# Value products of the second layer's first batch moved behind its last heads, more products of zeros before its norm, and the last FFN unit's factors put between a gate and its sum

## The reference, cut to what matters

```
h = layernorm(x) * (1 + ca) + sa
q = (h @ Wq.T + bq)            # 16 heads of 16
k = h @ Wk.T + bk              # one head of 16
v = h @ Wv.T + bv              # one head of 16
scores = q k^T * scale, masked to s < t; attn = softmax(scores); out = (attn v) @ Wo.T + bo
x = x + ga * out
h = layernorm(x) * (1 + cb) + sb
x = x + gb * (shared_ffn(h) + routed_ffn(h))
```

## Time and profile before

| What | Value |
|---|---|
| median of 3 runs | 636.39 us (634.04 to 637.16) |
| the profiled execution's own time | 634.54 us |
| its span, first to last instruction | 632.7 us |
| mean granted TensorE clock | 0.990 |
| busy share of PE, DVE, ACT | 93%, 58%, 46% |
| `filler` products of zeros (L703) | 28 in all |

### The profile page before, as it was taken

The page is one execution under the profiler, slowest core; times in us unless marked ns, Lnnn a source line. Parts: engine busy times, 40 slices in busy tenths (PEclk is TensorE's granted clock), DMA queues, the critical chain, the costliest instruction groups (busy, mean ns, idle before and its releaser), DMA issues.

```text
span 632.7 us, 10398 instructions
## 1 busy us (share of the span) xinstructions
PE 591.4 (93%) x3826; PEld 459.1 (73%) x3826; DVE 369.5 (58%) x725; ACT 291.6 (46%) x450; POOL 117.8 (19%) x90
## 2 busy tenths in 40 slices
PE   4898999998999999999999798889999999999995
PEld 3788645686898888888887465544447788888885
DVE  6477756755444545455557789893476523344456
ACT  3666775564323333333342563348763744333331
POOL 4400031223112222211230000003101331122220
PEclk9998999999999999999999799999999999999999
DMA  8464674000011111111100024402210000111101
GB/s 315 131 223 138 213 222 148 2 10 16 26 51 50 50 36 39 50 50 50 50 26 1 0 74 142 125 31 91 80 37 2 26 25 26 51 50 50 50 1 67
DMA packets 22195, 44.66 MB, mean 71 GB/s; under 512 B 3632, under 2 KB 7632, under 8 KB 22160
## 3 DMA queue, kind: packets, MB, share of 16 engines
q1 hardware_dynamic: 21840, 44.05, 21.9%
q10 hardware_dynamic: 320, 0.13, 0.1%
HBM read 33.16 MB, written 11.01 MB: 70 GB/s over the span
## 4 chain that ended last, share of the span: by engine, by line
PE 70%; DVE 19%; ACT 5%; DMA 2%; issue 2%; POOL 1%; SPq 0%; ACTq 0%; DVEq 0%
PE PS L559 33%; PE PS L1000 16%; DVE nmx L1606 6%; PE PS L883 4%; PE PS L852 2%; PE PS L720 2%; PE PS L718 2%; PE PS L831 2%; PE PS L836 2%; DVE stats L1493 2%; DVE x L1673 1%; DMA qk_slot<-rows_scr 1%; PE PS L898 1%; PE PS L597 1%; DVE xn L1818 1%
## 5 line engine op out<-in xcount | busy, mean ns | idle before, releaser
L1323 ACT ACTIVATE qk_hi<-xn 128x512 fp32r<-128x512 f32 x82 | 51.7, 631 | 166.6 <-DVE xn L1818 137.0
L559 PE MATMUL PS<-h_hi,wqkv_hi 128*128 128x512 f32 x304 | 103.0, 396 | 3.0 <-DVE h_lo L1527 2.2
L559 PE MATMUL PS<-h_hi,wqkv_lo 128*128 128x512 f32 x272 | 92.4, 396 | 1.8 <-DVE xn L1728 1.8
L1815 DVE TENSOR_TENSOR prs<-prs,PS 128x512 f32<-128x512 f32 x60 | 41.2, 687 | 84.7 <-PE PS L559 84.6
L525 POOL TENSOR_TENSOR wqkv_hi<-fw_raw,wqkv_hi 128x768 fp32r<-128x768 f32 x18 | 33.1, 1838 | 244.4 <-ACT wqkv_hi L1299 244.4
L1822 DVE TENSOR_TENSOR qk_lo<-xn,qk_hi 128x512 fp32r<-128x512 f32 x70 | 48.4, 692 | 50.3 <-ACT qk_hi L1323 50.3
L1319 ACT ACTIVATE prs<-PS 128x512 f32<-128x512 f32 x82 | 48.7, 594 | 49.5 <-PE PS L559 49.5
L559 PEld LDWEIGHTS PS<-h_hi,wqkv_hi 128*128 128x128 f32 x304 | 57.2, 188 | 15.3 <-DVE h_lo L1527 2.9
L559 PE MATMUL PS<-h_lo,wqkv_hi 128*128 128x512 f32 x160 | 62.9, 393 | 0.0
L559 PEld LDWEIGHTS PS<-h_hi,wqkv_lo 128*128 128x128 f32 x272 | 51.1, 188 | 13.3 <-DVE xn L1728 2.7
L1000 PE MATMUL PS<-wqkv_hi,qk_hi 128*128 128x256 f32 x280 | 52.1, 285 | 0.9 <-POOL qk_lo L531 0.7
(11 more groups left out here) (266 smaller groups left out, 1176.4 us busy)
## 6 DMA issues: line engine op xcount, KB each, us to landing
fw_raw<-in_ffn SPq DMA_DIRECT2D x41, 384.0 KB, 3.1
qk_slot<-rows_scr SPq DMA_DIRECT2D x32, 200.0 KB
rows_scr<-qk_hi SPq DMA_DIRECT2D x16, 256.0 KB
qk_slot<-q_scr SPq DMA_DIRECT2D x32, 100.0 KB
rows_scr<-qk_lo SPq DMA_DIRECT2D x8, 256.0 KB
wmod<-in_wmod SPq DMA_DIRECT2D x1, 1536.0 KB, 13.1
x<-in_x SPq DMA_DIRECT2D x2, 512.0 KB, 4.3
wmod<-in_wmod SPq DMA_DIRECT2D x1, 1024.0 KB, 9.4
```

Source lines behind the costliest of these rows:

```text
L559: ins = nc.tensor.matmul(dst, left(a, c), right(b, c), start=n == 0, stop=n == total - 1)
L1323: nc.scalar.activation(hidR[b][0], hid[b], ACT.Copy).then_inc(f["hi"], 1)
L1815: tt(hid[buf] if half is None else gu[buf], gact[buf], PS[:, 5, :], ALU.mult).then_inc(f["gu"], 1)
```

## The change

- `project1(0, 3)`, the 16 value products of batch 0, moves on PE from ahead of `project1(0, 0)` to behind `scores1(0, 6)`, and from bank 4 to bank 7. Bank 7 holds the value products of batch 1 by then, so it waits for `v1_taken` 1, which is now `take_v1(1)`. The wait for `v1_taken` 1 ahead of `scores1(0, 0)` goes.
- `take_v1(0)` on DVE moves from ahead of `q1_low(0, 0)` to behind `maxima1(0, 7)`. `take_v1(1)` stays behind `maxima1(0, 6)`. The wait of PE for `v1_taken` 2 ahead of `scores1(1, 0)` stays in its place.
- 12 products of zeros are made behind `project1(0, 2)`, ahead of the wait for `y_gated`; and those ahead of `norm_transposes(2, (0,))` go from 8 to 14.
- In layer 1 the factors of the last unit, `last_unit(3, 0)`, are made between the gate's product and the sum of `half_out(0, 1)` instead of behind the sum.

```diff
-        BANKS1 = ((1, 6, 0, 4), (7, 6, 6, 7))
-        PROJECTED1 = ((0, 2), (0, 3), (0, 0), (0, 1), (1, 2), (1, 0), (1, 1), (1, 3))
+        BANKS1 = ((1, 6, 0, 7), (7, 6, 6, 7))
+        PROJECTED1 = ((0, 2), (0, 0), (0, 1), (1, 2), (1, 0), (1, 1), (1, 3), (0, 3))
...
+                if (b, m) == (0, 3):
+                    pe.wait_ge(v1_taken, 1)
...
-                later = {0: (0, 1), 1: (1, 2), 2: (1, 0), 3: (1, 1), 4: (1, 3)}
+                later = {0: (0, 1), 1: (1, 2), 2: (1, 0), 3: (1, 1), 4: (1, 3), 6: (0, 3)}
                 project1(0, 2)
+                filler(12, 7)
                 pe.wait_ge(y_gated, 2 * B * 2)
-                project1(0, 3)
                 project1(0, 0)
...
-                    if j == 0:
-                        pe.wait_ge(v1_taken, 1)
-                    elif j == 2:
+                    if j == 2:
                         pe.wait_ge(qhi, 4 * B + 3)
...
-                    filler(8, 7)
+                    filler(14, 7)
                     norm_transposes(2, (0,))
...
-            def gate_and_add(l, which, b, i, bank):
+            def gate_and_add(l, which, b, i, bank, between=None):
...
                 tt(tmp, y, gate[:, l, which, b, :].unsqueeze(1).to_broadcast([P, 2, D]), ALU.mult).then_inc(y_gated, 1)
+                if between:
+                    between()
                 dve.wait_ge(y_gated, k + 1)
...
-                aggregate = half_out(0, 1)
+                aggregate = half_out(0, 1, lambda: last_unit(n + 1, 0) if l else None)
...
                 for k in range(n + 1, 2 * n):
-                    last_unit(k, 0)
+                    if not (l and k == n + 1):
+                        last_unit(k, 0)
                     last_unit(k, 1)
...
             q1_low(0, 2)
-            take_v1(0)
             q1_low(0, 0)
-                     5: lambda: q1_low(1, 1), 6: lambda: take_v1(1)}
+                     5: lambda: q1_low(1, 1), 6: lambda: take_v1(1), 7: lambda: take_v1(0)}
```

More of the change, by code:

```diff
@@ L1844, in ffn, with half_out @@
                     modulation1()
-                def half_out(b, i):
+                def half_out(b, i, between=None):
                     dve.wait_ge(f["w2"], 2 * TILES[l] - TAIL[l] * (1 - b))
-                    return gate_and_add(l, 1, b, i, 2 * b + i)
+                    return gate_and_add(l, 1, b, i, 2 * b + i, between)
                 def last_unit(k, part):
```

## The result

The changed kernel is slower: 643.23 us median of 9 runs (642.55 to 650.57) against 636.39 us of 9 runs (634.04 to 639.75), ratio 1.0119 with a 95% interval of 1.0086 to 1.0152. The forecast was 639.0, its range ended at 642.3.

The account below looks back on a forecast made before the run. It took the first row maximum's start, DVE at batch 0's end and PE's two gate groups to bound the kernel. -1.64 + 3.45 + 1.3 - 0.45 = +2.66 us on the median 636.39 gave 639.0, range 635.2 to 642.3.

Parts of the forecast that it names:

- What bounds the kernel: First row maximum's start, DVE at batch 0's end and PE's two gate groups decide; clock dips once, at the layers' seam.
- The seam, gain 1.64 us: Between the layers: zeros cost nothing and keep the clock up, so the first score comes 1.64 us earlier; bounds 0 and 3.1.
- The end of batch 0, loss 3.45 us: Two v1_taken waits: DVE idles 2.3 us before step 7's maxima, and `gates1(0)` starts 3.45 us later; bounds 2.3 and 3.7.
- The clock at the end of batch 0, loss 1.3 us, from 0 to 4: PE waits and narrow products there bring a clock fall: 0.6 us in step 7, 0.7 in the next scores.
- T: End of `take_v1(1)`, batch 1's value step on DVE; 391.09 us in the kernel before.
- The last unit, gain 0.45 us: At the kernel's end: the last unit's factor, made ahead of the sum, starts 0.45 us earlier; bounds 0 and 0.69.
- number 2: Clock falls at batch 0's end and stays down through scores and gates: 3.9 for 1.3, +5.3 us, 641.7; chance 0.13.
- Numbers 1 and 3: 1: stall but clock stays up, +1.36 us, 637.8, chance 0.22. 3: seam still dips, +4.3 us, 640.7, chance 0.12.
- number 4: Seam's dip costs more without the profiler, gain up to 4.95 us: 635.7, or 634.4 without the clock term; chance 0.08.
- the clock's upper bound of 3.9 us: Batch 0's end, low clock outlasting scores and gates: 0.6 + 1.7 + 1.6 us for feeding step 7, scores and gates.
- The sum: Whole kernel: seam, batch 0's end, clock and last unit together give +2.66 us.
- only idle time counts: Reading of the skill's gap warning: the clock term at batch 0's end would be nothing and the sum +1.36 us.

Follow-up runs that it names:

- E7: Changed kernel without the 12 products of zeros and with 8 in place of 14, move and last unit kept; 648.22 us in its one run.
- E2: Changed kernel with 12 and 8 products of zeros added ahead of PE's two waits for v1_taken; median 638.93 us, ratio 1.0052 to the kernel before.
- E4: Changed kernel with only batch 1's value step on DVE one step earlier; median 638.68 us, ratio 1.0026 to the kernel before.
- E3: Changed kernel with both value steps on DVE one step earlier, PE's order kept; median 635.95 us, ratio 1.0012 to the kernel before.
- E5: Changed kernel with the move alone undone, zeros and last unit kept; median 635.86 us, ratio 0.9956 to the kernel before.
- E10: Changed kernel run a third time without edit, for its profile; 641.65 us at a mean clock of 0.986.
- E1: Changed kernel run again without edit, for a second profile; median 642.42 us, ratio 1.011 to the kernel before.
- E9: Changed kernel with the move undone and 4 and 5 zeros around the value products for the 12; median 636.61 us, ratio 0.996 to before.

## Why the prediction was wrong

- **What bounds the kernel**: right. The seam, DVE's maxima and the two gate groups behind them decided it. The clock doesn't dip once in the earlier trace rows, though: slice 4 reads 8 too, the dip of rows 9.
- **The seam, gain 1.64 us**: right, 1.62 to 1.64 in every kernel with the zeros; the transposes of batch 1 were what came late next, as said. E7 shows that the zeros did it.
- **The end of batch 0, loss 3.45 us**: right in mechanism and nearly in size. E2, the same waits at the full clock, measured 3.77, a little over the top bound of 3.7: the hole was 2.39 and not 2.28 us, the four pieces took 1.83 us up to the gates and not 1.7, and the rest, 0.1, lies in the steps from one engine to the next. E4 shows the first wait's hole gone with the first value step earlier, E3 both.
- **The clock at the end of batch 0, loss 1.3 us, from 0 to 4**: this is the step that failed. That the clock would fall was right, when and what it would cost wasn't: 2.67 and 2.77 us in two profiles and 5.09 in the third. The prediction put the fall near T + 1, behind a wait and part of the value products. It came at T + 0.45, T - 0.2 and T - 0.5, the last two with PE idle and no narrow product yet made; so the 4.5 us of waiting and narrow products that it reckoned with weren't needed. It also left the 16 value products at 1.76 us. They took 3.14, 3.41 and 3.40, against 1.81 in E2: 1.3 to 1.6 us more. It gave the feeding of step 7's maxima 0.6 us; it was 0.3 at the first and 0.9 over the four (405.18 to 409.16, 3.98 us instead of E2's 3.05). In the first profile these make 2.57 of the 2.67. Its 1.3 us then took the fall to hold for half of the next group. In the third profile it held through the second wait, `scores1(1, 0)` (1.5 us more) and part of the gates (0.6 more), 13.7 us in all.
- **The last unit, gain 0.45 us**: right, 0.37 to 0.45 us in eight of the nine profiles with it; the last stretch of the ninth, E5's, has a dip of its own.
- **The rivals**: number 2, the long fall, was the nearest, at 641.7 us with a chance of 0.13; it lacked the value products too. Numbers 1 and 3 are in none of the three profiles of the changed kernel, and number 4, the faster one, did not occur. The range ended 0.9 us under the measured median. Against E10 the clock's upper bound of 3.9 us was 1.2 too low: 1.6 for the value products and 0.6 for the feeding were missing, and the gates were put 1.0 too high.
- **The sum**: predicted -1.64 + 3.45 + 1.3 - 0.45 = +2.7. Measured by stretches, with E10 for the changed kernel and E2 for its split: -1.64 + 3.77 + 5.09 - 0.37 = +6.85; by the medians +6.84. With the 2.67 us of the first profile the sum is +4.4 us, or 640.8 on the median, which lies in the range. So the clock term was too small in every profile, but that its long form is what took the median out of the range rests on E10 alone.
- **The rule on idle gaps** ("TensorE: Matmul & The Clock Gate" of the Trainium skill, "Why this matters for your kernels"): its warning against gaps agrees with the fall in the wait of 2.89 us here, and with E7's at the seam, which came in 3.75 us of idle PE. E3 speaks against the reading that only idle time counts: its clock fell with PE busy in every window from 388 us on, behind products of 16 columns, where the kernel before had more idle time and no fall. That is one execution.

What stays open: how the dips are spread over the executions of one kernel. Three profiles of the changed kernel show 6.8, 6.8 and 13.7 us at the end of batch 0, and the timed runs of all kernels differ by several microseconds, in part with their mean clock. The dip at the seam isn't in every execution of the kernel before either: one took 632.78 us at a mean clock of 0.999, where 6.8 us at half clock would by my estimate leave 0.995 at most. And the start differs before the clock falls at all: layer 0's first row maximum came at 26.59 us in E1's profile, 26.86 before, 28.10 in E10's and 30.25 in E7's.

## What to carry to other kernels

Before moving a small step, ask what its two waits will stand in front of in each queue. Here 1.8 us of PE work and 0.2 us of DVE work, which E5 shows to be free where they were, became a round trip between two engines that had run a step apart, at 3.8 us, and let the clock fall for 2.7 to 5.1 more. When a stall on TensorE is priced, everything that stands behind it in the queue has to be priced at the lower clock too, narrow products included. And zeros beside narrow products gave all that the move was to give: E9 keeps the order of before and is 0.4% faster than it.

## What the runs showed of the hardware

- Sixteen fp32 products of 16 columns took 1.76 us at 2.4 GHz and 393.35 - 389.95 = 3.40 us at 1.2 GHz (L696 in E10). They nearly double, like wide ones.
- The clock fell behind such products with PE busy (E3, 389 to 391 us), and stayed up when 4 and 5 products of zeros of 512 columns stood on either side of them (E9). With bf16 products of zeros in PE's waits it stayed at full, at the seam in eight profiles and at the end of batch 0 in E2; without them it fell (E7, and the changed kernel).
- The same program had dips of quite different length: 3.4 us in layer 0 in E1's profile and 30.7 us in the first one of the changed kernel, which moved the seam from 356.23 to 369.06 us. Stretches between two marks of the trace, without a dip or with the same one, agreed to 0.1 us or better where the medians needed a dozen runs to tell 0.4%.
